# One table set for logarithms and exponentials on ScalarE, and a new order of every engine's calls, in a decoder layer on one core

## The reference

```python
x = x + attn(_layernorm(x))     # 16 heads of 32, one K and V head, rope, K and V rounded to 8 bits,
                                # windows of 128 every 64: sigmoid(scores), divided by their sum, blended
x = x + wkv(w, u, _layernorm(x), ctx_2048)          # keys: the normed x; values: ctx
x = x + ffn(_layernorm(x))      # tokens and weights quantised; silu(gate) * up, rms norm, quantised, down

def step(carry, kv_t):          # wkv, along the 256 tokens
    p, q, o = carry
    kt, vt = kv_t
    no = jnp.maximum(o, u + kt)
    A = jnp.exp(o - no)
    E = jnp.exp(u + kt - no)
    y = (A * p + E * vt) / (A * q + E)
    ...
```

## Time and profile before

| | us |
|---|---|
| median of 3 runs (lowest, highest) | 1096.42 (1095.57, 1097.88) |
| the profiled execution | 1100.16 |
| its span, first to last instruction | 1098.8 |
| busy: TensorE, VectorE, ScalarE, GpSimd | 878.8, 844.1, 706.2, 435.7 |

### The profile page before, as it was taken

How to read it: one execution, slowest core, us unless ns; L and a number is a source line. 1 busy time by engine, 2 the same in 40 slices (tenths; PEclk the granted TensorE clock), 3 DMA queues, 4 the chain that set the end, 5 groups by cost and what they waited for, 6 DMA issues and landing times.

```text
span 1098.8 us, 22051 instructions
## 1 busy us (share of the span) xinstructions
PE 878.8 (80%) x8388; PEld 516.9 (47%) x8388; DVE 844.1 (77%) x1630; ACT 706.2 (64%) x1179; POOL 435.7 (40%) x494
## 2 busy tenths in 40 slices
PE   5883656678888888888888888989898888886665
PEld 2342545445454555555545555555455555553222
DVE  4744477887888888888887888888877888876953
ACT  0114737276868686868777777777786868684633
POOL 2100113236263635353535453535454444444522
PEclk9986776869999999999999999999999999997878
DMA  8876424020515151515142524242424343212022
GB/s 328 314 231 246 151 100 148 19 85 10 103 59 103 55 107 54 107 51 99 63 95 67 84 78 84 78 84 79 84 78 72 91 67 95 68 59 40 28 59 67
DMA packets 125754, 106.90 MB, mean 97 GB/s; under 512 B 99312, under 2 KB 101088, under 8 KB 124496
## 3 DMA queue, kind: packets, MB, share of 16 engines
q1 hardware_dynamic: 119344, 101.47, 35.6%
q0 software_dynamic: 624, 2.59, 0.7%
q10 hardware_dynamic: 5680, 1.42, 0.6%
HBM read 65.62 MB, written 10.49 MB: 69 GB/s over the span
## 4 chain that ended last, share of the span: by engine, by line
ACT 30%; PE 26%; DVE 20%; issue 15%; SPq 5%; DMA 2%; POOL 2%; DVEq 0%; ACTq 0%; POOLq 0%
PE bank L508 9%; ACT arena L734 6%; PE bank L607 5%; PE bank L527 4%; ACT L786 3%; ACT sums L741 3%; DVE junk L1160 3%; PE bank L597 3%; ACT sums L746 2%; ACT junk L786 2%; ACT junk L791 2%; DVE amax L1126 2%; DVE fs L1169 2%; ACT L757 2%; ACT L734 2%
## 5 line engine op out<-in xcount | busy, mean ns | idle before, releaser
L597 PE MATMUL bank<-w_up_gate,qT 128*128 128x512 bf16 x1024 | 244.9, 389 | 40.4 <-ACT junk L786 20.6
L1364 POOL TENSOR_TENSOR work<-junk,lnw 128x512 f32<-128x512 f32 x128 | 188.3, 1491 | 126.0 <-DVE junk L1160 111.7
L1347 POOL TENSOR_TENSOR sums<-sums,blend 128x448 f32<-128x448 f32 x64 | 73.6, 1170 | 274.2 <-ACT sums L746 274.2
L597 PEld LDWEIGHTS bank<-w_up_gate,qT 128*128 128x128 bf16 x1024 | 97.2, 100 | 155.8 <-ACT junk L786 26.3
L508 PE MATMUL bank<-wide,wq_sb 128*128 128x256 f32 x512 | 120.8, 397 | 34.8 <-DVE rows L1061 30.8
L607 PE MATMUL bank<-w_down,work 128*128 128x512 bf16 x512 | 132.0, 408 | 19.8 <-ACT junk L786 10.5
L508 PEld LDWEIGHTS bank<-wide,wq_sb 128*128 128x128 f32 x512 | 100.6, 199 | 61.2 <-issue 46.9
L734 ACT ACTIVATE arena<-bank 128x384 f32<-128x384 f32 x256 | 104.9, 497 | 36.0 <-PE bank L527 35.8
L527 PE MATMUL bank<-wide,k_win 32*128 32x128 f32 x1536 | 69.7, 317 | 72.9 <-ACT arena L734 54.2
L786 ACT ACTIVATE junk<-bank,deq 128x512 f32<-128x512 f32 x128 | 86.3, 686 | 54.0 <-PE bank L597 52.2
L559 PE MATMUL bank<-wo_sb,wide 128*128 128x512 f32 x256 | 115.8, 607 | 2.6 <-DVE wide L1054 2.6
(11 more groups left out here) (150 smaller groups left out, 1536.9 us busy)
## 6 DMA issues: line engine op xcount, KB each, us to landing
sums<-in_xT SPq DMA_DIRECT2D x8, 1024.0 KB, 11.2
wide<-in_xT SPq DMA_DIRECT2D x16, 512.0 KB, 3.8
rows<-in_x SPq DMA_DIRECT2D x16, 512.0 KB, 4.9
ctx_T<-in_ctxT SPq DMA_DIRECT2D x16, 512.0 KB, 3.7
wide<-wide SPq DMA_DIRECT2D x64, 128.0 KB, 2.0
out<-rows SPq DMA_DIRECT2D x32, 256.0 KB, 2.1
kv_b<-k_raw SPq DMA_DIRECT2D x16, 384.0 KB
work<-in_wgT SPq DMA_DIRECT2D x4, 1024.0 KB, 16.4
```

Of the source, the lines that this page charges most:

```text
L597: last = te.matmul(bank[4 + k % 4][:, :], qT[:, c, t * P:(t + 1) * P], w_up_gate[:, m, c, cols], start=c == 0, stop=c == NC - 1)
L1364: ge.tensor_tensor(hid_w[:, t, cols], hid[:, n % 2, :], lnw[:, cols], op=ALU.mult).then_inc(z_set.sem, 1)
```

## The change

`log_tables()` puts an explicit ACT_TABLE_LOAD into ScalarE's program, for the table set with the id 6. [...] Then all calls of a round are placed in another order, on all five engines; no call is added or taken away beside `log_tables()`. The main moves in a steady round:

- ScalarE: each `inverses` and `wkv_inverses` right behind or near its logarithm, instead of in groups; both `scale_hidden` ahead of `silu(f,0,0)` and behind `scale_tokens`; the last two silus and three squares of a batch, and `scale_tokens`, in the next round's first place behind `set_keys`.
- TensorE: `gate_up(f,0,3)` ahead of `scores(b,0)`; `down(g,1,0)` ahead of `scores(b,3)`; `down(g,1,1)` between `dens`; `gate_up(f,1,0)` ahead of `dens(b,3)`, `gate_up(f,1,1)` behind `nums(b,3)`.
- VectorE: `join`, `output(.,0)` and `peak(.,0)` behind `keys_grid` of the next sequence; both `hidden_scale` together; `hidden_round` ahead of `rope`, `rotate` later.
- SP: `next_queries` ahead of `next_keys`, both ahead of `turn_hidden(g,1,0)`; the `store`s behind these; `turn_hidden(g,0,0)` at the end of the round before.
- The blocks of `round_weights`, `sum_weights` and `load_weights` at other places of rounds 0 to 2.

```diff
+LN_EXP = 6
 ... sync_program
             if do_b:
                 turn_queries(b, 0)
-            if do_g:
-                turn_hidden(g, 0, 0)
-            if do_b:
                 turn_queries(b, 1)
+            if i == 1:
+                load_weights(DOWN, 1)
             if do_g:
                 turn_hidden(g, 0, 1)
+            if i == 1:
+                load_weights(DOWN, 2)
+            if do_g:
+                turn_hidden(g, 1, 1)
+            if do_b:
+                next_queries(b)
             if i == 0:
                 load_weights(UP, 0)
-            if i == 1:
-                load_weights(DOWN, 1)
+            if do_b:
+                next_keys(b)
             if do_g:
                 turn_hidden(g, 1, 0)
-            if do_b:
-                next_keys(b)
-            if do_g:
-                turn_hidden(g, 1, 1)
-                store(g, 0)
-            if do_b:
-                next_queries(b)
...
+            if do_f:
+                turn_hidden(f, 0, 0)
 ... tensor_program
+                gate_up(f, 0, 3)
             if do_b:
                 scores(b, 0)
-            if do_f:
-                gate_up(f, 0, 3)
...
                 scores(b, 2)
+            if do_g:
+                down(g, 1, 0)
+            if do_b:
                 scores(b, 3)
-            if do_g:
-                down(g, 1, 0)
-            if do_b:
                 dens(b, 0)
+            if do_g:
+                down(g, 1, 1)
+            if do_b:
                 dens(b, 1)
                 dens(b, 2)
                 nums(b, 0)
...
 ... scalar_program
+        def log_tables():
+            se.add_instruction(mybir.InstLoadActFuncSet(name=nc.get_next_instruction_name(),
+                                                        engine=mybir.EngineType.Activation, act_func_set_id=LN_EXP))
...
+            if do_f:
+                scale_tokens(f)
+            if do_g:
+                scale_hidden(g, 0)
                 scale_hidden(g, 1)
             if do_f:
                 silu(f, 0, 0)
             if do_w:
+                log_tables()
                 exps(w)
...
                 probs(b, 3)
+                log_tables()
+                logs(b, 0)
+                inverses(b, 0)
             if do_w:
                 wkv_logs(w, 0)
-            if do_b:
-                logs(b, 0)
-            if do_w:
+                wkv_inverses(w, 0)
                 wkv_logs(w, 1)
             if do_b:
                 logs(b, 1)
-            if do_w:
-                wkv_inverses(w, 0)
-            if do_b:
-                inverses(b, 0)
-                inverses(b, 1)
             if do_w:
                 wkv_inverses(w, 1)
             if i == 0:
                 sum_weights(UP, 1)
             if do_b:
+                inverses(b, 1)
                 logs(b, 2)
+                inverses(b, 2)
                 logs(b, 3)
-                inverses(b, 2)
-                inverses(b, 3)
             if i == 1:
                 sum_weights(DOWN, 2)
+            if do_b:
+                inverses(b, 3)
...
 ... vector_program
+            if do_g:
+                hidden_scale(g, 0)
+                hidden_scale(g, 1)
             if i == 2:
                 round_weights(DOWN, 1)
             if do_g:
-                hidden_scale(g, 1)
+                hidden_round(g, 0)
             if do_b:
                 rope(b, 0)
             if do_g:
-                hidden_round(g, 0)
+                hidden_round(g, 1)
+            if do_b:
+                rope(b, 1)
...
-            if do_w:
-                join(w)
-            if do_g:
-                output(g, 0)
-            if do_f:
-                peak(f, 0)
```

More of the change, by code:

```diff
@@ L427, in sync_program @@
                 turn_tokens(w)
+            if i == 0:
+                load_weights(UP, 3)
+            if do_f:
+                turn_hidden(f, 0, 0)
+            if i == 0:
+                load_weights(DOWN, 0)
         for t in range(NT):
@@ L641, in tensor_program @@
             if do_b:
+                scores(b, 3)
                 dens(b, 0)
+            if do_g:
+                down(g, 1, 1)
+            if do_b:
                 dens(b, 1)
@@ L801, in scalar_program @@
                 set_keys(b)
+            if i == 2:
+                sum_weights(DOWN, 3)
+            if i == 0:
+                sum_weights(GATE, 3)
             if do_g:
+                silu(g, 1, 2)
+                squares(g, 1, 1)
+                silu(g, 1, 3)
+                squares(g, 1, 2)
+                squares(g, 1, 3)
+            if do_f:
+                scale_tokens(f)
+            if do_g:
+                scale_hidden(g, 0)
                 scale_hidden(g, 1)
@@ L810, in scalar_program @@
                 squares(f, 0, 0)
-            if i == 0:
-                sum_weights(GATE, 3)
+            if i == 1:
+                sum_weights(DOWN, 0)
             if do_f:
@@ L818, in scalar_program @@
                 probs(b, 0)
+            if i == 1:
+                sum_weights(DOWN, 1)
             if do_f:
@@ L822, in scalar_program @@
                 probs(b, 1)
-                probs(b, 2)
             if do_f:
                 squares(f, 0, 3)
-            if i == 1:
-                sum_weights(DOWN, 1)
+            if do_b:
+                probs(b, 2)
             if i == 0:
@@ L860, in scalar_program @@
                 sum_weights(UP, 2)
+            if i == 0:
+                sum_weights(UP, 3)
             if do_f:
                 squares(f, 1, 0)
[L863 to L876, removed]
-                sum_weights(DOWN, 0)
     def vector_program(ve):
@@ L1204, in vector_program @@
                 keys_grid(b)
-            if i == 2:
-                round_weights(UP, 3)
+            if do_f:
+                join(f)
+            if i == 1:
+                round_weights(GATE, 3)
+            if do_h:
+                output(h, 0)
+            if do_g:
+                peak(g, 0)
+            if do_h:
+                output(h, 1)
             if do_f:
                 refine(f, 0)
-            if do_h:
-                output(h, 1)
+                refine(f, 1)
             if do_w:
                 blend_windows(w, 0)
-                blend_windows(w, 1)
             if do_f:
-                refine(f, 1)
                 quotient(f, 0)
             if do_w:
+                blend_windows(w, 1)
                 blend_windows(w, 2)
@@ L1247, in vector_program @@
             if i == 2:
-                round_weights(DOWN, 0)
+                weight_mean(DOWN)
             if do_f:
@@ L1281, in vector_program @@
             if i == 2:
+                round_weights(DOWN, 2)
+            if do_b:
+                rotate(b, 0)
+            if i == 2:
                 round_weights(DOWN, 3)
-            if i == 0:
-                round_weights(GATE, 1)
-            if do_w:
-                values(w)
-            if do_f:
-                hidden(f, 0, 2)
             if do_b:
```

88 lines of the change are left out of this document (36 added, 52 removed).

## The result

The changed kernel takes 1122.85 us in the median (1120.35 to 1130.34) against 1097.15 for the kernel before on the same chip: a ratio of 1.0243, 95% interval 1.0191 to 1.0296. It is slower, as the likeliest case of the forecast said (slower and faster had a chance of 0.45 each), but by 26 us, not by 7, and outside its range, which ended at 1114. That it is slower is clear of the interval; that it is by more than 2% is not.

The account below looks back on a forecast made before the run. No engine is full, so the order of work sets the pace. 12 x (57.5 - 56.3) = +14, with -4, -3 and 0 for the ends, makes +7: 1103 us on the median's scale, range 1055 to 1114.

Parts of the forecast that it names:

- the likeliest case of the forecast: Whole kernel: the stall comes as forecast, 1103 us, own range 1090 to 1113; chance 0.55, of which 0.35 slower.
- the stall of down(g,1,0): TensorE ahead of down(g,1,0): stands still from 24.3 to 27.7 of the round, waiting for its transpose behind two loads.
- the head: Rounds 0 to 2, which have no down: together -4 us, bounds -12 and +5.
- The reads: ScalarE: three table reads on the path go, 3.9 us a round; it wins 3.1 to 3.5 net.
- TensorE behind the last scores: From scores(b,3) to the next queries: 26.1 us where it was 29.15, so 3.1 won.
- my 1.5: SP's queue: delay of the transpose's landing by the 512 KB queries load in front, between 0 and 3.8 us.
- The clock: TensorE around the standstill: granted-clock dips cost 0.9 us a round, bounds 0 and 1.9.
- my rival with the clock at 0.50 every round: More than the stall: landing at 29 or this clock, 58.5 us a round, 1116 in all; chance 0.07.
- keys_grid behind the scan: VectorE: keys_grid(b+1) at 25.7 instead of 30.4, up to 2 us of stall waiting for keys, hidden.
- I had -1: Round 1, hanging on GpSimd's 7.6 us wait: rounding DOWN 0 leaves the chain, -1 us.
- the tail: Round 15 without the stall, as it loads no next queries or keys: -3 us; after it, together 0.
- No stall: Rival: the transpose overtakes the loads or these are quick; rounds of 53.6, 1057 us with the ends; chance 0.20.

Follow-up runs that it names:

- experiment 3: The kernel before in its old order, with one log_tables() ahead of the first wkv_logs, three reads less a round: 1111.62 us, ratio 1.0134.
- experiment 10: Experiment 3 with GpSimd's weigh_windows and outputs narrowed to 8 columns: 1064.77 us, ratio 0.9703.
- experiment 11: The kernel before with GpSimd's weigh_windows and outputs narrowed to 8 columns, reads kept: 1101.39 us, ratio 1.0034.
- experiment 5: Experiment 2 with three more log_tables() in the group behind probs(b,3): 1138.28 us, ratio 1.0369.
- experiment 8: The changed kernel with next_keys moved behind turn_hidden(g,1,0), next_queries left in front: 1131.44 us, ratio 1.0307.
- experiment 2: The changed kernel with next_queries moved from ahead of next_keys to behind turn_hidden(g,1,0): 1075.04 us, ratio 0.9808.
- experiment 13: Experiment 12 with join ahead of keys_grid on VectorE: 1067.65 us, ratio 0.9730.
- experiment 1: The changed kernel with turn_hidden(g,1,0) and turn_hidden(g,1,1) swapped in SP's queue: 1083.94 us, ratio 0.9887.
- experiment 6: The changed kernel with the SP queue moves of experiment 1 and experiment 2 together: 1083.87 us, ratio 0.9878.
- experiment 12: Experiment 6 with six filler matmuls on TensorE behind attention_out(b,1): 1069.52 us, ratio 0.9744.
- experiment 4: The changed kernel with 15 unused matmuls between the two waits of down(g,1,0): 1107.55 us, ratio 1.0105.

## Why the forecast was wrong

The mechanism that the forecast bet on, the stall of down(g,1,0), came as described; what failed were sizes: the step between landing and matmul, which I had left out, the clock behind the stall, and the head, where I had -4 us and the run shows +1.8.

**The reads** hold. Rounds 3 to 14 have ScalarE busy 458.40 us, before 505.26: 3.9 less a round, as summed. But that the reads lay on the path of before, which I read from the chain, gave them no price there: experiments 3, 10 and 11 show that in the old order VectorE, stretched beside GpSimd, takes the time over at once. What gives the gain here is the new order, and in it the reads are worth 4.07 (experiment 5).

**TensorE behind the last scores** holds: 25.63 from the end of scores(b,3) to the next queries, forecast 26.1 (its terms add up to 26.0).

**The stall** holds in kind and nearly in size. The issue came at 19.77 (19.8). The landing took 8.08 where my terms made 7.9; 0.5 us pass between landing and the first matmul, which I had left out. So down starts at 28.36 and not at 27.7. What the two loads do to the transpose can now be set side by side, the longest landing of a round, in the mean of the twelve rounds of each kernel: 4.7 us behind the queries alone (experiment 8; 4.3 to 5.9), 7.4 behind the keys alone (2; 6.9 to 7.8), 8.1 behind both (7.5 to 8.8), and 2.8 behind neither. The queries cost 1.9 by themselves and 0.7 on top of the keys, on either side of my 1.5. The keys' two loads, of fewer bytes, cost 4.6; 1476 of the 1732 packets in that stretch (636.7 to 647.0) are under 512 B, but no run shows whether their size is the reason.

**The clock** is a term that was mis-sized. I took 0.9 a round in all, of which before has 0.6 in its mean. Between the changed kernel and experiment 2 the same matmuls differ by 1.28, in TensorE's busy time alone; filling the stall gave back 1.5 in the mean and 2.1 in the typical round. The low clock fell in every round on down(g,1,0), which took 3.04 to 3.19 us in all twelve and held up everything; that was my rival with the clock at 0.50 every round. I gave it 0.07 and ended the range under its 1116, which was itself too low.

A round is thus 28.36 + 4.05 + 25.63 = 58.04 where I had 30.5 + 26.1 + 0.9 = 57.5, and the mean 58.17: +22.6 instead of +14. By terms, the start of down is 0.7 late (0.5 of it the step between landing and first matmul, at nothing in my sum), the clock over down and scores(b,3) is 1.25 for 0.9, and the stretch behind gives 0.5 back: over twelve rounds +8, +4 and -6 us.

**keys_grid behind the scan** is hidden in steady rounds but not in round 1. This step failed outright, and cost 4 us: I had priced the order of keys_grid and join for steady rounds alone, and nothing of it went into round 1. VectorE and ScalarE there:

```profile
172.01 0.65 DVE L1027 TENSOR_SCALAR kv_b<-kv_b,grid 128x256 f32<-128x256 f32 x2 [3.19 <-DMA kv_b<-v_raw]
```
```profile
176.99 0.63 ACT L756 ACTIVATE sums<-sums 128x512 f32<-128x512 f32 x1 [3.39 <-DVE sums L1094]
```

The keys' load stands behind DOWN's 1 MB loads in SP's queue; join and wkv_logs wait with keys_grid, and with them GpSimd's last product, which ends at 186.75, 46.6 of the round, where before had it at 43.2; the all-reduce that round 1 hangs on the earlier trace rows starts 6.0 behind that end in both. Round 1 took 65.45 us for 62.41 before, and I had -1. With the first queries 1.6 later, round 0 at -3.2 and round 2 at +0.4 the head came to +1.8 for my -4, inside its bounds. Experiment 13's round 1 is 3.2 shorter with join in front. The tail was -1.0 for -3.

Together: the median is 19.8 us over the forecast's 1103. Of that 8.6 are the rounds, 5.8 the head and 2.0 the tail, and some 3 are that the profiled execution of before lay 3.7 above its median and that of the changed kernel only 0.6. So no single term made the miss: the direction came from the stall, which was forecast, and the size from the head, the rounds and the tail together.

**The rivals.** No stall would have been 1057 by my sum, from rounds of 53.6; with the stall out of the way the runs give 53.5 to 54.6 and 1067 to 1084 (experiments 1, 2, 6, 12 and 13, the last two with filler). The round was nearly right, the ends were not. The reads were saved: 84 in the whole program, where I had about 80.

## What to carry over

A chain of waits says what ended last, not what its removal brings: ask what the work behind it will run beside. Here VectorE's tensor_tensor and scalar_tensor_tensor of 128x512 took 0.69 and 0.68 us alone, and 1.62 and 1.68 where they met GpSimd's. In a DMA queue price a transfer by its issue, by what has to be waited for ahead of it (without next_queries ahead the issue came 2.1 us earlier here), and by every load in front, not by its bytes alone (432 KB of keys cost 4.6 us here, 512 KB of queries 1.9); where two transfers are wanted, give the first place to the one whose consumer is wanted first, and check the other's consumer too. A standstill of TensorE cost here, beside itself, the low clock on the work behind it (in every round on the down behind the stall of 3.4 to 4.5 us, 3.17 us for 1.90; ahead of the queries, in some rounds behind 2.2 us and in none behind 1.6), so that useless matmuls in it paid: 15 us in experiment 4, 14 in experiment 12.

## Not expected of the hardware

- Six useless matmuls (1.3 us) ahead of the queries took 1.1 us off each round (54.57 to 53.49), and left the granted clock at 1.00 over twelve rounds. The standstill that they shorten was only 2.2 us in most rounds, and 0.9 of it is left; in experiment 2, where it is 1.6 in most, the clock was 0.99 without them.
- VectorE's tensor_tensor of 128x512 took 0.69 us alone and 1.62 beside GpSimd, its mean over the program 1195 ns in place of 725.
- A transposing DMA of 2.8 us landed in 4.7 in the mean behind a load of 512 KB and in 7.4 behind one of 384 and one of 48 KB.
